# A fused MetaFormer block on one core: PSUM read once for two copies of the hidden layer, gate ranks moved, another prologue, and six of seven normalised rows made on GpSimd with their halves one slot later

## The reference, cut to what matters

```python
x = x + conv(_ln_c(x))          # super-token attention, cells of 8 x 8 pixels
t = _to_tokens(x)               # 12544 tokens of 96 channels
t = t + ffn(_ln_t(t))           # mixture of 4 experts, 2 of them taken
...
# conv, per image: 49 cells; each pixel against the 9 cells around its own
aff = softmax(einsum('bnpc,bnck->bnpk', pix, sf9) * scale)
sft = fold3(einsum('bnpc,bnpk->bnck', pix, aff)) / (aff_sum + 1e-12)
attn = softmax(einsum('bhdn,bhdm->bhnm', k, q) * hd ** -0.5, axis=-2)   # 8 heads over 49 cells
pix_out = einsum('bnck,bnpk->bncp', unfold3(proj(attention)), aff)
...
# ffn
masked = probs * mask; masked = masked / (sum(masked) + 1e-9)
h = gelu(einsum('bsd,edh->ebsh', x, w1) + b1)       # exact gelu, 96 -> 384, for all four experts
y = einsum('ebsh,ehd->ebsd', h, w2) + b2            # 384 -> 96
out = einsum('bse,ebsd->bsd', masked, y)
```

## Time and profile before

| | us |
|---|---|
| median of three runs | 581.5 (579.17 to 582.25) |
| profiled execution | 581.49 |
| its span, first to last instruction | 579.7 |
| PE busy | 539.2 (93%) |
| DVE busy | 442.9 (76%) |
| ACT busy | 365.2 (63%) |
| GpSimd busy | 106.7 (18%) |
| mean granted TensorE clock | 0.935 of full |

### The profile page before, as it was taken

One profiled execution on the slowest core, in us unless ns is written; L12 is line 12 of the kernel. 1 busy time (PEld: TensorE's weight loads), 2 busy tenths in 40 slices (PEclk: granted clock), 3 DMA queues, 4 the chain that ended last, 5 costly groups with the idle time before them and its releaser, 6 DMA issues.

```text
span 579.7 us, 15701 instructions
## 1 busy us (share of the span) xinstructions
PE 539.2 (93%) x6612; PEld 415.3 (72%) x6612; DVE 442.9 (76%) x1208; ACT 365.2 (63%) x379; POOL 106.7 (18%) x191
## 2 busy tenths in 40 slices
PE   8897869999999998999999998999999989999995
PEld 4895747787687875787687875787677766777774
DVE  6574766888669897988669897867689798777775
ACT  1043235866767476866767476866777787777773
POOL 3230001126000240226000240220000621103100
PEclk9657557999999998999999998999999989999999
DMA  9942003000000001200000000000000000000000
GB/s 215 241 108 78 2 2 83 14 2 13 14 3 13 14 14 48 62 2 13 14 2 14 14 13 14 14 1 14 14 13 15 15 1 14 15 13 14 13 15 24
DMA packets 15596, 17.50 MB, mean 30 GB/s; under 512 B 13781, under 2 KB 13917, under 8 KB 15134
## 3 DMA queue, kind: packets, MB, share of 16 engines
q1 hardware_dynamic: 14498, 14.76, 10.4%
q10 hardware_dynamic: 1028, 1.74, 1.3%
HBM read 11.68 MB, written 4.82 MB: 28 GB/s over the span
## 4 chain that ended last, share of the span: by engine, by line
PE 63%; DVE 11%; ACT 11%; issue 8%; DMA 4%; POOL 2%; ACTq 1%; DVEq 0%
PE ps L1159 23%; PE ps L1174 13%; PE ps L1179 6%; PE ps L1015 5%; ACT h L551 4%; PE ps L1026 4%; DMA gate_bb<-gate_b 4%; ACT hh L543 4%; PE ps L999 3%; DVE xt L877 2%; PE ps L1168 2%; DVE hl L864 2%; PE ps L1114 2%; DVE st L759 1%; DVE pden L727 1%
## 5 line engine op out<-in xcount | busy, mean ns | idle before, releaser
L543 ACT ACTIVATE hh<-ps 128x1344 f16<-128x1344 f32 x112 | 144.6, 1292 | 90.3 <-PE ps L1159 89.1
L864 DVE TENSOR_TENSOR hl<-h,hh 128x1344 f16<-128x1344 f32 x112 | 177.3, 1583 | 19.5 <-ACT h L551 18.7
L1159 PE MATMUL ps<-xhl,w_hi 97*128 97x448 f16 x672 | 187.1, 361 | 2.8 <-ACT xhl L510 1.9
L877 DVE SCALAR_TENSOR_TENSOR xt<-ps,gl,xt 112x96 f32<-112x96 f32 x448 | 110.7, 309 | 55.7 <-PE ps L1179 55.5
L551 ACT ACTIVATE h<-ps 128x1344 f32<-128x1344 f32 x112 | 144.3, 1288 | 0.0
L1174 PE MATMUL ps<-w_lo,hh 128*128 128x96 f16 x1344 | 129.6, 207 | 0.0
L1174 PE MATMUL ps<-w_hi,hh 128*128 128x96 f16 x1344 | 129.4, 207 | 0.0
L1174 PEld LDWEIGHTS ps<-w_lo,hh 128*128 128x128 f16 x1344 | 116.9, 98 | 7.6 <-issue 0.2
L1174 PEld LDWEIGHTS ps<-w_hi,hh 128*128 128x128 f16 x1344 | 118.4, 99 | 3.9 <-issue 0.2
L1159 PE MATMUL ps<-xhl,w_lo 97*128 97x448 f16 x336 | 120.6, 359 | 0.0
L364 POOL TENSOR_TENSOR x<-xs,x 112x384 f16<-112x384 f32 x28 | 35.8, 1277 | 327.7 <-ACT x L504 327.7
(11 more groups left out here) (163 smaller groups left out, 493.3 us busy)
## 6 DMA issues: line engine op xcount, KB each, us to landing
xt<-xtok SPq DMA_DIRECT2D x8, 624.8 KB, 13.5
xch<-x SPq DMA_DIRECT2D x4, 1176.0 KB, 7.5
out<-xt SPq DMA_DIRECT2D x28, 168.0 KB, 2.3
h<-w ACTq DMA_DIRECT2D x2, 576.0 KB
wqkv_sb<-wqkv ACTq DMA_DIRECT2D x1, 228.0 KB
tab<-table ACTq DMA_DIRECT2D x1, 119.5 KB, 5.7
xch<-cells ACTq DMA_DIRECT2D x1, 85.8 KB
projx_sb<-projx ACTq DMA_DIRECT2D x1, 36.4 KB, 13.0
```

The lines of the kernel that those rows point to most:

```text
L543: act.activation(hh[:, i % 3, :, 0:UT], z, ACT.Gelu, scale=1.0 / WS).then_inc(S["hh_ready"], 1)
L864: dve.tensor_tensor(hl[:, i % 2, :, 0:UT], h32[:, i % 2, :, :], hh[:, i % 3, :, 0:UT], ALU.subtract).then_inc(S["hl_ready"], 1)
L877: ins = dve.scalar_tensor_tensor(out=xt[:, b, t, 0:C], in0=ps[0:PT, Y, j * C:(j + 1) * C], scalar=gl[:, b % 2, t, e:e + 1], in1=xt[:, b, t ...
L1159: ins = pe.matmul(ps[:, CH * (i % 2) + c, 0:UT], ww[:, w0:w0 + 128], xhl[:, b % 2, half, r * UT:(r + 1) * UT], start=(n == 0), stop=(n == 2))
```

## The change

- `hidden_full` now comes first and is the only one that reads z. `hidden_high` copies h32 to float16 behind it, after a wait for it.
- `normalise` of rows 1 to 6 goes to GpSimd (row 1 of image 0, and row 0 of each, stay on DVE). For rows 2 to 6 it stands in the slots of `NORMAL`; `tokens_high` and `tokens_low` of these rows stand one slot later. Row 1 of the next image is normalised in slot 25 and its low half moves to slot 26.
- `gate_ranks` in slot 26 stands ahead of `low_part`.
- In the slots ACT makes 1 - tanh for the attention's weights with a second operation, where DVE had it. For image 0 the weights are one exponential.
- Two loads of tables of functions go from the prologue. On DVE, `variance` and `newton_step` are fused to fewer instructions.
- Twelve `keep_busy` products stand ahead of TRN 0 of image 0 and eight behind it.

`TABLE`, `NORMAL` and `BEFORE` are as they were.

```diff
@@ variance
-            s.mark(s.engine.tensor_tensor(m[:, 2, :], m[:, 0, :], m[:, 0, :], ALU.mult))
+            if s.engine is nc.vector:
+                s.mark(s.engine.scalar_tensor_tensor(out=m[:, 2, :], in0=m[:, 0, :], scalar=0.25, in1=m[:, 0, :],
+                                                     op0=ALU.mult, op1=ALU.mult))
+            else:
+                s.link(s.engine.tensor_tensor(m[:, 2, :], m[:, 0, :], m[:, 0, :], ALU.mult))
+                s.mark(s.engine.tensor_scalar(m[:, 2, :], m[:, 2, :], 0.25, None, ALU.mult))
             s.link(s.engine.tensor_scalar(m[:, 1, :], m[:, 1, :], 1.0 / C, eps, ALU.mult, ALU.add))
-            s.link(s.engine.tensor_scalar(m[:, 2, :], m[:, 2, :], 0.25, None, ALU.mult))
@@ newton_step
-            s.link(s.engine.tensor_tensor(t[:, 1, :], t[:, 0, :], v, ALU.mult))
-            s.link(s.engine.tensor_scalar(t[:, 1, :], t[:, 1, :], -0.5, 1.5, ALU.mult, ALU.add))
-            s.link(s.engine.tensor_tensor(y, t[:, 1, :], y, ALU.mult))
+            if s.engine is nc.vector:
+                s.link(s.engine.scalar_tensor_tensor(out=t[:, 1, :], in0=t[:, 0, :], scalar=-0.5, in1=v, op0=ALU.mult,
+                                                     op1=ALU.mult))
+                s.link(s.engine.scalar_tensor_tensor(out=y, in0=t[:, 1, :], scalar=1.5, in1=y, op0=ALU.add,
+                                                     op1=ALU.mult))
...
@@ gpsimd
+            def normalise(b, r):
+                pool.wait_ge(S["norm_ready"], b + 1)
+                pool.wait_ge(S["xs_ready"], b * G + r)
+                if b > 0:
+                    pool.wait_ge(S["xhi_ready"], (b - 1) * G + r + 1)
+                    pool.wait_ge(S["xlo_ready"], (b - 1) * G + r + 1)
+                for t in range(r * TU, (r + 1) * TU):
+                    ins = pool.tensor_scalar(xs[:, t, :], xt[:, b, t, 0:C], rstd2[:, t:t + 1], mr[:, t:t + 1], ALU.mult,
+                                             ALU.add)
+                ins.then_inc(S["xs_ready"], 1)
...
                     if slot in NORMAL:
-                        tokens_low(b, NORMAL[slot])
+                        normalise(b, NORMAL[slot])
+                    if slot - 1 in NORMAL:
+                        tokens_low(b, NORMAL[slot - 1])
...
-                        if slot in (24, 25):
-                            tokens_low(b + 1, slot - 24)
+                        if slot == 24:
+                            tokens_low(b + 1, 0)
+                        if slot == 25:
+                            normalise(b + 1, 1)
+                        if slot == 26:
+                            tokens_low(b + 1, 1)
@@ scalar
+                act.wait_ge(S["prob_tanh"], 2 * b - 1)
+                act.activation(pden[:], prob[:], ACT.Copy, bias=1.0, scale=-1.0).then_inc(S["prob_tanh"], 1)
+
+            def first_attention():
+                act.wait_ge(S["side_dve"], reads_up_to((0, "SCO", 0)))
+                act.activation(prob[:], prob[:], ACT.Exp, scale=float(HD) ** -0.5).then_inc(S["prob_ready"], 1)
...
-                act.activation(hh[:, i % 3, :, 0:UT], z, ACT.Gelu, scale=1.0 / WS).then_inc(S["hh_ready"], 1)
...
+            def hidden_high(i):
+                act.wait_ge(S["h_ready"], i + 1)
...
+                act.copy(hh[:, i % 3, :, 0:UT], h32[:, i % 2, :, :]).then_inc(S["hh_ready"], 1)
...
-            act.activation(scrap[:, 3:4], scrap[:, 0:1], ACT.Gelu)
...
-            attention_tanh(0)
+            first_attention()
...
-            act.activation(scrap[:, 4:5], scrap[:, 0:1], ACT.Exp)
...
                 if i + 2 < ALL:
+                    hidden_full(i + 2)
                     hidden_high(i + 2)
-                    hidden_full(i + 2)
-                if slot in NORMAL:
-                    tokens_high(b, NORMAL[slot])
+                if slot - 1 in NORMAL:
+                    tokens_high(b, NORMAL[slot - 1])
@@ vector
-                at.link(dve.tensor_scalar(pden[:], prob[:], -1.0, 1.0, ALU.mult, ALU.add))
...
-            attention_weights(0)
...
+                if b + 1 < B and slot == 26:
+                    gate_ranks(b + 1)
                 if i + 1 < ALL:
                     low_part(i + 1)
...
-                if slot in NORMAL:
-                    normalise(b, NORMAL[slot])
...
-                    if slot == 25:
-                        normalise(b + 1, 1)
-                    if slot == 26:
-                        gate_ranks(b + 1)
@@ tensor
+                if v == (0, "TRN", 0):
+                    keep_busy(12)
                 side(v)
+                if v == (0, "TRN", 0):
+                    keep_busy(8)
```

More of the change, by code:

```diff
@@ L305, in newton_step @@
             s.link(s.engine.tensor_tensor(t[:, 0, :], y, y, ALU.mult))
-            s.link(s.engine.tensor_tensor(t[:, 1, :], t[:, 0, :], v, ALU.mult))
-            s.link(s.engine.tensor_scalar(t[:, 1, :], t[:, 1, :], -0.5, 1.5, ALU.mult, ALU.add))
-            s.link(s.engine.tensor_tensor(y, t[:, 1, :], y, ALU.mult))
+            if s.engine is nc.vector:
[3 more added lines that the diff above has]
+                                                     op1=ALU.mult))
+            else:
+                s.link(s.engine.tensor_tensor(t[:, 1, :], t[:, 0, :], v, ALU.mult))
+                s.link(s.engine.tensor_scalar(t[:, 1, :], t[:, 1, :], -0.5, 1.5, ALU.mult, ALU.add))
+                s.link(s.engine.tensor_tensor(y, t[:, 1, :], y, ALU.mult))
         @block.sync
@@ L534, in side_read, with hidden_full @@
                     tokens_turned(b, k)
-            def hidden_high(i):
+            def hidden_full(i):
                 z = ps[:, CH * (i % 2):CH * (i % 2) + CH, 0:UT]
                 act.wait_ge(S["z_done"], i + 1)
[L539 to L542, removed]
-                act.activation(hh[:, i % 3, :, 0:UT], z, ACT.Gelu, scale=1.0 / WS).then_inc(S["hh_ready"], 1)
-            def hidden_full(i):
-                z = ps[:, CH * (i % 2):CH * (i % 2) + CH, 0:UT]
                 if i < 2:
@@ L551, in hidden_full @@
                 act.activation(h32[:, i % 2, :, :], z, ACT.Gelu, scale=1.0 / WS).then_inc(S["h_ready"], 1)
+            def hidden_high(i):
+                act.wait_ge(S["h_ready"], i + 1)
+                if i == 0:
+                    act.wait_ge(S["pool_set"], 8)
+                if i >= 3:
+                    act.wait_ge(S["y_done"], i - 2)
+                act.copy(hh[:, i % 3, :, 0:UT], h32[:, i % 2, :, :]).then_inc(S["hh_ready"], 1)
             cells_centred(0)
@@ L574, in _ @@
             tokens_turned(0, 0)
+            hidden_full(0)
             hidden_high(0)
-            hidden_full(0)
             tokens_high(0, 1)
+            hidden_full(1)
             hidden_high(1)
-            hidden_full(1)
             for i in range(ALL):
@@ L723, in attention_weights @@
             def attention_weights(b):
-                dve.wait_ge(S["prob_tanh"], b + 1)
-                at.link(dve.tensor_scalar(pden[:], prob[:], -1.0, 1.0, ALU.mult, ALU.add))
+                dve.wait_ge(S["prob_tanh"], 2 * b)
                 at.link(dve.reciprocal(pden[:], pden[:]))
```

## The result

| | before | changed |
|---|---|---|
| median of the runs, us | 581.9 (4 runs) | 589.4 (4 runs, 588.5 to 591.0) |
| ratio, 95% interval | | 1.012 [1.008, 1.017] |
| profiled execution, us | 581.5 | 588.5 |
| span, us | 579.7 | 586.7 |
| PE / DVE / ACT / GpSimd busy | 93 / 76 / 63 / 18% | 93 / 71 / 64 / 29% |

The time lies inside the range and beside rival B's number (590); the likeliest case, no measurable change (583.5), is not what happened. One run of e4 (610.7 us), over 1.5% above the fastest of its kernel, is in the slow state and left out. Busy shares say nothing of the cause: VectorE lost 25 us of work, GpSimd took 65 on, and the time went up.

The account below looks back on a forecast made before the run. The body was taken as bound by PE's own instructions, with holes and the half clock behind them to gain: 581.5 - 6.9 - 5.3 - 2.0 + 12.8 + 3.3 = 583.4, said as 583.5 us, range 575.5 to 591.

Parts of the forecast that it names:

- rival B: Slower, 590 us: all four TRN 4 holes cost a half-clock piece and the prologue's clock falls anyway; chance 0.22.
- the likeliest case: Whole kernel: gains and new stalls nearly cancel, 583.5 us, own range 578.6 to 584.4; chance 0.38.
- prologue: Start of the kernel: fused statistics, exponential alone, kept clock and filling products save 6.9 us.
- z read once: Hidden layer on ACT: copying hh from h costs nothing but 0.15 us in whatever follows on ACT.
- ranks moved, rows 1 off DVE: Changes of image: ranks fall into DVE's idle time, saving 1.9 us at two and 1.5 at the last, 5.3 in all.
- DVE relieved: Slots where DVE was late: normalising on GpSimd gives back 2.0 us in sum.
- halves a slot later, waiting: Turns of rows 4 and 2: late low halves make PE wait, 12.8 us over four images.
- clock behind the new holes: Behind the new holes: half-clock pieces of 1.7 us, bounds none and four, two taken, 3.3 us.
- halves and clock together: Turns of rows 4 and 2: waiting of 12.8 and half clock of 3.3 us, together 16.1.
- about 6: Turns of rows 4 and 2: the 12.8 us of waiting if each low half took 0.91, unhindered by VectorE.
- GpSimd against DVE: Slot 6: the low affinities start ahead of hl and may slow it, nothing to 1.0 us in three images; nothing taken.
- rival C: Slower, 586.5 us: DVE waits for GpSimd, whose low affinities and normalising hold hl, 3 us more; chance 0.16.

Follow-up runs that it names:

- e4: The kernel before with only the fp16 halves of rows 2 to 6 made a slot after normalising, still on VectorE: 600.7 us, 1.030 of before.
- e6: The kernel before with the new prologue alone: 577.0 us, 0.990 of before.
- e7: The kernel before with the single read of z alone (h from PSUM, hh copied from h): 588.2 us, 1.008 of before.
- e9: The kernel of e1 with z read twice by ScalarE, as before the change: 567.4 us, 0.973 of before.
- e11: The kernel before with only the next image's gate ranks moved ahead of the hidden layer's lower part in slot 26: 578.0 us, 0.991 of before.
- e5: The kernel of e1 with the normalising of rows 1 to 6 back on VectorE: 578.2 us.
- e8: The changed kernel with 9 to 12 filling products ahead of row 4's turn in each image, 10 at row 2's in image 0: 583.3 us.
- e12: The changed kernel with VectorE's lower hidden part in slot 14 waiting for GpSimd's lower half of row 4: 579.0 us, 0.992 of before.
- e1: The changed kernel with the halves of rows 2 to 6 back in their row's slot, GpSimd still normalising: 569.8 us, 0.980 of before.
- e2: The changed kernel with only row 4's halves back in slot 11: 576.5 us.

## Why the prediction was right in its range and wrong in its likeliest case

| term | predicted | measured | by |
|---|---|---|---|
| prologue | -6.9 | -6.0 alone; -8.2 between the two traces, 1.9 of it the throw behind TRN 0 | e6 |
| z read once | 0 | +5.2 alone; 0.18 at each of 20 places, 3.6, against e1 | e7, e9 |
| ranks moved, rows 1 off DVE | -5.3 | ranks alone -6.2 (-5.7 by their places in the trace); in the changed trace -1.9, -1.8, 0 | e11 |
| DVE relieved | -2.0 | normalising on GpSimd, rows 1 included, about -4 | e5 |
| halves a slot later, waiting | +12.8 | +12.3 (below) | traces |
| clock behind the new holes | +3.3 | +8.5, five pieces of 1.7 | traces, e8, e12 |
| halves and clock together | +16.1 | +19.6 undone by medians, 16.1 by traces; +18.4 alone | e1, e4 |

**The step that failed was the clock.** It is the term of 3.3 in the sum, and its size was wrong, not its mechanism. The prediction weighed nought to four pieces and took two, "as the holes are a little shorter" than one of 2.35. All four of TRN 4 took one, behind idle times of 2.39 three times and 1.79. Four were rival B's term, and a fifth, at TRN 2 of image 0, was in no case. Three pieces too few are 5.2 us, against the 5.9 by which the forecast was missed. That this matches so well is in part luck, for the other errors nearly cancel. Between the two traces the prologue brought 1.3 more than it was given and slots 15 to 21 brought 1.1 more; the changes of image brought 1.7 less, and the waits for AFT's copy, 1.7 in all, were in no sum. It is luck, too, that the result lies beside rival B's number. The other half of B, the prologue's clock falling at 51.5 as before, did not happen: the clock stood at 1.00 from 41.2 to 57.0, then fell for 17 us.

```profile
41.20:57.00 15.80, 13.29 (x150) 10.51 (x149) 7.85 (x18) 6.51 (x13) 1.82 (x1) 1.00 0.35 93
57.20:74.20 17.00, 15.18 (x88) 12.79 (x88) 16.07 (x73) 2.73 (x7) 0.91 (x1) 0.50 0.01 1
74.30:84.40 10.10, 10.10 (x83) 7.96 (x81) 4.56 (x14) 6.42 (x6) 3.74 (x5) 1.00 0.01 2
```

**The mechanism was right where it cost most.** The replay from the earlier trace rows gave slot 13 a delay of 2.25 in images 0 to 2 and 1.9 in image 3. Less the piece of 1.7, the steps are 2.0, 2.0, 2.0 and 1.9. The collision of GpSimd's lower half with hl, ending 0.78 after it, was found as read: 156.28 against 155.50. The prediction put the cost of the collision at about half of the 12.8; e12 shows 0.95 of waiting for each TRN 4 and, because the hole then stays short, the clock as well. Row 2 came out at 1.06 instead of 1.0 in images 1 to 3. Together with image 0's 2.9 less its piece, the waiting adds up to 2.0 x 3 + 1.9 + 1.06 x 3 + 1.2 = 12.3 against 12.8, and with five pieces to 20.8. Undoing the part brought 19.6 by medians and 16.1 by traces (e1). The prediction's "about 6" for low halves that aren't held stays half tested: e12 takes back 3.8 of the 12.3 at TRN 4, and no run frees TRN 2's halves. 20 of the 28 low halves took 0.91 before, not half of them.

**z read once was mis-sized.** The 0.15 "in whatever follows on ACT" was seen, and the pair measured 0.19 longer. But it was priced at nothing because PE doesn't wait for z or hh. What follows on ACT is the copies of AFT and TRN, and PE does wait for those: the earlier trace rows has the line, with 0.28 idle ended by ACT's affT. A delay on a queue costs at every wait for what stands behind it in that queue, not only at waits for the delayed result. The same holds for the 1 - tanh that moved to ACT: it takes 0.37 ahead of AFT's copy, and of the 0.58 that slot 9 costs, 0.40 is left in e9, where z is read twice. No run took it out alone.

```profile
133.58 0.37 ACT L507 ACTIVATE pden<-prob 128x196 f32<-128x196 f32 x1
133.85 0.88 ACT L495 COPY affT<-ps 96x896 f16<-96x896 f16 x1
...
134.88 0.57 PE L1061 MATMUL ps<-ident,aff 112*96 112x112 f16 x8 [1.27 <-ACT affT L495]
```

**Changes of image.** The waits became 1.23 and one alike behind the next first layer, without half clock, as predicted (1.3), and gave 1.9 and 1.8 where 1.9 each was said. The last one gave nothing instead of 1.5: there PE waits 1.72 for TRN 0 of image 3, whose row comes out of GpSimd's deviation, and a half-clock piece follows as before. In e9 and e11 the same wait is 1.60 and no piece follows; there this change of image gives back 1.6 and 1.2.

```profile
221.14 0.34 PE L1193 MATMUL ps<-b_hl,ones 128*128 128x384 f16 x1 [1.23 <-DVE xt L907]
...
469.20 0.57 PE L1139 MATMUL ps<-ident,x 112*96 112x112 f16 x8 [1.72 <-issue]
470.19 0.42 PE L1193 MATMUL ps<-b_hl,ones 128*128 128x384 f16 x1 [0.43 <-DVE xt L907]
```

**Prologue.** PE's turn of the probabilities starts at 49.87 and takes 0.64, as said (50.2, 0.64). From there to the end of the projection it is 4.9 us where it was 8.35: 3.4 gained, the prediction's upper bound, where it took 3.0. The last 2.5 of the 8.2 come behind the start of TRN 0, where 0.5 was given, and of these 1.9 are the throw told at e6. A single pair of traces can't give the gain of a start closely: the same prologue ended its first second layer 3.4 us later in e1's profiled execution than in that of the changed kernel.

**GpSimd against DVE.** hl didn't grow: 1583 ns on the mean before, 1562 after. The page's line of the group:

```profile
L894 DVE TENSOR_TENSOR hl<-h,hh 128x1344 f16<-128x1344 f32 x112 | 175.0, 1562 | 20.8 <-issue 17.5
...
L377 POOL TENSOR_SCALAR xs<-xt,rstd,mr 112x96 f32<-112x96 f32 x92 | 58.9, 652 | 0.0
```

So rival C is out. GpSimd is the one that pays. Its normalising of 96 elements takes 0.418 at the median and 2.25 at most, where VectorE's took 0.322, and it is hidden as predicted. The Trainium skill (GPSIMD Engine Reference, Engine selection) puts the two at about the same rate for one input; here GpSimd takes 1.3 times as long at the median and twice as long on the mean.

**What stays open.** What decides in which of the two clusters an execution with the new prologue falls. Against the changed kernel's trace, e1's loses 1.5 ahead of TRN 0 and 2.0 behind it, and against e9's 1.9 in slots 3 and 4 of image 0; that would be most of the 6 us, but no trace of its lower cluster is there to show it. Open, too, is why one and the same hole is sometimes followed by half clock and sometimes not (next section).

## What to carry to other kernels

When a producer is moved a slot later, replay it against the consumer's fixed place; if the consumer is an otherwise dense TensorE, price each new hole of about 2 us at its length plus the half-clock piece behind it, here 1.7 us, and count those pieces in full, not by half (18 of the 19 holes of 2.09 us and more in these traces had one). Time each edit of a bundle alone: here the prologue, the ranks and GpSimd's normalising gained 6, 6 and 4 us, the later halves lost 16 to 20 and the single read 4 to 5, and undoing those two turned 1.2% slower into 2.7% faster. When one engine holds another up and has slack itself, making it wait (e12) can be the cheapest cure.

## What the runs showed of the hardware

- The clock follows holes in otherwise dense work closely: at TRN 4, idle times of 2.39 and 1.79 were each followed by 3.2 to 3.3 us at 0.50, one of 1.45 was not, and a hole of the same place filled with products of ones was not either. Over all fourteen traces, behind the first two second layers: of the 19 idle times of PE of 2.09 to 2.96 us, 18 were followed by a piece at half clock (e2's of 2.84 was not); of the 20 of 1.60 to 1.84, 15; of the 26 of 1.26 to 1.45, none.
- It isn't the hole's length alone. In e11 a hole of 0.66 in slot 19, as long as before's, was followed by lower clock, and slot 19 cost 1.6 more in images 0 and 1; in the kernel before it kept the full clock. In e7 the two holes of slot 19 were 0.88 and 0.87, and only the second was followed by lower clock. The first window is of e11, the second of before, each 2.1 us behind the end of that hole:

```profile
192.20:195.60 3.40, 3.40 (x44) 3.21 (x43) 1.55 (x9) 0.00 (x0) 0.00 (x0) 0.61 0.02 5
```

```profile
189.20:192.60 3.40, 3.40 (x49) 2.65 (x45) 2.93 (x12) 0.16 (x1) 0.00 (x0) 1.00 0.07 15
```

- A lower half of 0.91 us on GpSimd that starts 0.5 behind hl on VectorE takes 1.86 and ends 0.78 after it; started alone it takes 0.91. Of the 28, 8 took over 1.3 us before, 16 in the changed kernel and 12 in e12, where row 4's four are back at 0.91.
